# A two-layer graph network kernel: the second self weight's magnitudes are read earlier, and layer 1's self updates are put ahead of other vector work

## What is computed

```
deg_inv = 1 / max(deg, 1)                                  # deg: edges that arrive at a node
layer(h, Ws, Wn, b) = h @ Ws + (segment_sum(h[src], dst) * deg_inv[:, None]) @ Wn + b
h   = relu(layer(x, Ws0, Wn0, b0))
out = layer(h, Ws1, Wn1, b1)
result = layernorm(x + out)
```

## Time and profile before

| | |
|---|---|
| median of 3 runs | 699.4 us |
| profiled execution, device time | 701.54 us |
| its span, first to last instruction | 699.9 us |
| TensorE busy | 635.0 us (91%) |
| VectorE busy | 497.0 us (71%) |
| ScalarE busy | 274.1 us (39%) |
| GpSimd busy | 117.6 us (17%) |
| mean granted TensorE clock | 0.967 of full |

### The profile page before, as it was taken

One profiled execution on the slowest core, in us unless ns is written; L12 is line 12 of the kernel. 1 busy time (PEld: TensorE's weight loads), 2 busy tenths in 40 slices (PEclk: granted clock), 3 DMA queues, 4 the chain that ended last, 5 costly groups with the idle time before them and its releaser, 6 DMA issues.

```text
span 699.9 us, 11077 instructions
## 1 busy us (share of the span) xinstructions
PE 635.0 (91%) x3286; PEld 325.6 (47%) x3286; DVE 497.0 (71%) x1209; ACT 274.1 (39%) x492; POOL 117.6 (17%) x200
## 2 busy tenths in 40 slices
PE   3688989998999999999998999999979879879795
PEld 3644545544666666555554444444434334333242
DVE  7796487868777875398999866632029996676764
ACT  5572734343334344036444544423215331222221
POOL 3001236533233333100000000002121220000000
PEclk9799999999999999999999999999998989999998
DMA  8614000000000000333111000007724526100111
GB/s 316 236 63 178 1 1 0 0 1 1 0 1 1 0 0 0 117 126 120 60 60 32 0 1 1 0 1 248 264 91 150 178 86 242 61 31 30 61 60 54
DMA packets 16141, 50.33 MB, mean 72 GB/s; under 512 B 2616, under 2 KB 2776, under 8 KB 16096
## 3 DMA queue, kind: packets, MB, share of 16 engines
q1 hardware_dynamic: 16096, 49.77, 20.2%
HBM read 40.45 MB, written 9.31 MB: 71 GB/s over the span
## 4 chain that ended last, share of the span: by engine, by line
PE 58%; DVE 19%; issue 9%; DMA 5%; ACT 5%; SPq 1%; POOL 1%; DVEq 0%; POOLq 0%; ACTq 0%
PE ps L674 15%; PE ps L771 14%; PE ps L713 12%; PE ps L647 10%; PE ps L571 4%; DMA ws<-in_L_gnn_W_neigh 2%; DVE xz L1365 2%; ACT wn L966 2%; DMA wn<-in_L_gnn_W_self 2%; PE ps L808 2%; DVE table L1358 2%; DVE table L1340 2%; DVE wn L308 1%; DVE wn L1531 1%; DVE wn L1373 1%
## 5 line engine op out<-in xcount | busy, mean ns | idle before, releaser
L771 PE MATMUL ps<-xz,wn 128*128 128x512 f16 x600 | 137.3, 389 | 11.9 <-DVE ws L1531 6.2
L647 PE MATMUL ps<-wn,xz 128*128 128x512 f16 x480 | 116.4, 382 | 2.8 <-DVE wn L308 1.4
L674 PE MATMUL ps<-xz,ws 128*128 128x420 f16 (+1 forms) x576 | 116.1, 339 | 0.0
L836 ACT ACTIVATE scratch<-ps 128x240 uint16<-128x240 f32 x160 | 59.0, 371 | 120.3 <-PE ps L571 101.9
L1129 DVE TENSOR_SCALAR lohot<-iota_lo,table 125x128 f16<-125x128 f16 x320 | 87.8, 274 | 25.2 <-PE ps L571 24.6
L1131 DVE TENSOR_SCALAR scratch<-iota_q,table 125x240 f16<-125x240 f16 x320 | 104.5, 327 | 0.3 <-issue 0.2
L771 PEld LDWEIGHTS ps<-xz,wn 128*128 128x128 f16 x600 | 59.5, 100 | 87.3 <-DVE wn L1373 11.7
L485 POOL TENSOR_TENSOR A<-A,scratch 128x120 int32 x160 | 72.8, 455 | 138.9 <-ACT scratch L836 110.1
L808 PE MATMUL ps<-wn,A 128*128 128x512 f16 x200 | 79.1, 396 | 11.6 <-DVE scratch L1472 11.6
L713 PE MATMUL ps<-A,zh 128*128 128x420 f16 (+1 forms) x480 | 84.7, 340 | 0.0
L808 PE MATMUL ps<-ws,A 128*128 128x512 f16 x200 | 78.9, 394 | 0.0
(11 more groups left out here) (177 smaller groups left out, 658.4 us busy)
## 6 DMA issues: line engine op xcount, KB each, us to landing
ws<-in_L_gnn_W_neigh SPq DMA_DIRECT2D x16, 512.0 KB, 4.5
wn<-in_L_gnn_W_self SPq DMA_DIRECT2D x16, 512.0 KB, 5.0
zh<-in_x SPq DMA_DIRECT2D x9, 512.0 KB, 8.6
scratch<-in_x SPq DMA_DIRECT2D x9, 512.0 KB, 6.3
ws<-in_L_gnn_W_neigh SPq DMA_DIRECT2D x4, 1024.0 KB, 17.8
ws<-in_L_gnn_W_self SPq DMA_DIRECT2D x4, 1024.0 KB, 8.7
partial<-scratch SPq DMA_DIRECT2D x8, 512.0 KB, 3.8
wn<-partial SPq DMA_DIRECT2D x4, 512.0 KB, 6.9
```

Of the source, the lines that this page charges most:

```text
L647: ins = pe.matmul(ps[0:TP, 2 * r + half, :], lhs(a, k, t), w[:, k, b, half * HD:(half + 1) * HD], start=(k == 0 and a == 0 and b == 0), st ...
L674: ins = pe.matmul(ps[:, b, 0:CH[n]], ws[:, k, a, bass.ds(f * P, P)], xT[h][:, k, CO[n]:CO[n] + CH[n]], start=(k == 0 and a == 0 and h == 0 ...
L771: ins = pe.matmul(ps[:, b, :], slot[:, k, a, :], Tm[m][:, k, w, :], start=(m in (1, 2, 5) and k == 0 and a == 0 and w == 0), stop=(k == HK ...
L836: act.activation(stage[0:TP, r], ps[0:TP, 8 - banks + r % banks, 0:HN].rearrange("p (j w) -> p j w", j=JT), ACT.Copy).then_inc(counts_copi ...
```

## The change

Ws1's magnitudes are read in layer 0's aggregation, by eight loads of 512 KB into a buffer of their own, one at a time, and eight pairs of half-row sums on ScalarE, in every second unit from unit 4 on. tensor_max and scale("ws1") move into units 20 and 22, spread(3) stands right behind spread(2) on GpSimd, ahead of the memsets of h's tail. Layer 1's aggregation loses the magnitude reads (loads u = 0 to 3 and weight_sums(1, k)) and has the factor blocks from tile 0 on: t_sum4 behind tiles 0, 2, 4, 6, t_lows behind tiles 1, 3, 5, 7. In the self products the update of y comes before item_lows, finish is cut into `moments` (up to the variance) and the rest, which runs one iteration later; ScalarE's part is cut in the same way.

```diff
         def load_raw(eng, phase, u):
             slot, k = u % 2, u % HK
-            if 2 <= u < HK + 2:
-                eng.wait_ge(max_done, 2 * (HK * phase + u - 1))
+            if phase == 0 and 2 <= u < HK + 2:
+                eng.wait_ge(max_done, 2 * (u - 1))
             elif u >= HK + 2:
                 eng.wait_ge(t_low, ITEMS * (HK * phase + u - HK - 1))
...
+        def load_ws1(eng, k):
+            if k:
+                eng.wait_ge(ws1_summed, 2 * k)
+            eng.dma_start(ws1raw, Ws1[k * P:(k + 1) * P, :]).then_inc(ws1_in, 16)
# SyncE
             for u in range(2):
                 load_raw(sp, 0, u)
+            load_ws1(sp, 0)
...
                 for u in {0: (2, 3), 1: (4, 5), 3: (6,), 5: (7,)}.get(f, ()):
                     load_raw(sp, 0, u)
+                for k in {1: (1,), 2: (2, 3), 3: (4,), 4: (5,), 5: (6, 7)}.get(f, ()):
+                    load_ws1(sp, k)
...
-            for u in range(2):
+            for u in range(HK, HK + 2):
                 load_raw(sp, 1, u)
             sp.wait_ge(z_low, 4 * IT)
             for n in range(2):
                 load_x(n)
-            for u in range(2, HK):
-                load_raw(sp, 1, u)
...
-                for u in {0: (4, 5), 3: (6,), 4: (7,)}.get(n, ()):
+                for u in {1: (6,), 3: (7,)}.get(n, ()):
                     load_raw(sp, 1, u)
                 load_x(n + 2)
# GpSimd
             spread(2)
+            spread(3)
...
-            for n in range(3):
-                residual(n)
-            spread(3)
-            for n in range(3, JT):
+            for n in range(JT):
                 residual(n)
# ScalarE
+            def ws1_sums(k):
+                act.wait_ge(ws1_in, 16 * (k + 1))
+                for a in range(2):
+                    m = MC["ws1"] + 2 * k + a
+                    act.activation(ws1dump, ws1raw[:, a * HD:(a + 1) * HD], ACT.Abs,
+                                   accum_out=mx[:, m:m + 1]).then_inc(ws1_summed, 1)
+                    act.wait_ge(ws1_summed, 2 * k + a + 1)
...
                     for k in {(0, 0): (0,), (0, 1): (1,), (1, 0): (2,), (1, 1): (3,)}.get((f, n), ()):
                         weight_sums(0, k, unread)
+                    if q >= -2 and q % 2 == 0 and q < 2 * KT - 2:
+                        ws1_sums(q // 2 + 1)
...
             for k in range(HK):
-                weight_sums(1, k, unread)
-            act.wait_ge(scale_ready, 6)
-            for k in range(HK):
                 for i in range(ITEMS):
                     t_item(1, k, i)
...
-                if m == (3 if p < IT - 1 else 2):
-                    finish(2 * p)
-                if m == 4:
-                    finish(2 * p + 1)
+                if e and e - 1 in ROW7:
+                    normalize(ROW7[e - 1])
+                if e in ROW7:
+                    root(ROW7[e])
+            normalize(JT - 1)
# VectorE
+                    if (f, n) == (6, 2):
+                        dve.wait_ge(ws1_summed, 2 * KT)
+                        tensor_max("ws1", 2 * KT, MC["ws1"])
+                    if (f, n) == (7, 1):
+                        scale("ws1")
+                        signal(scale_ready)
...
             for n in range(JT):
                 y_tile(n)
-                if n == 1:
-                    dve.wait_ge(max_done, 4 * HK)
-                    tensor_max("ws1", KT, MC["ws1"])
-                if n == 2:
-                    scale("ws1")
-                    signal(scale_ready)
+                if n == 0:
                     mul("cs1", "p_h", "p_ws1", 2.0 ** -25)
-                if 3 <= n < 3 + HK:
+                if n < 2 * HK and n % 2 == 0:
                     for i in range(4):
-                        t_sum4(1, n - 3, i)
-                    t_lows(1, n - 3, range(ITEMS))
-                if n == JT - 2:
+                        t_sum4(1, n // 2, i)
+                if n < 2 * HK and n % 2 == 1:
+                    t_lows(1, n // 2, range(ITEMS))
+                if n == 2 * HK - 1:
                     dve.wait_ge(t_low, 2 * ITEMS * HK)
                     for e in range(ITEMS):
                         s_sum(1, e)
+                if n == JT - 2:
                     for e in range(ITEMS):
                         item_lows(1, e)
...
                 if e + ITEMS < NP7:
                     s_sum(1, e + ITEMS)
-                    item_lows(1, e + ITEMS)
+                if e == NP7 - 1:
+                    finish(JT - 2)
...   # wait for product e, y += product e, statistics of the half row
-                if m == (3 if p < IT - 1 else 2):
-                    finish(2 * p)
-                if m == 4:
-                    finish(2 * p + 1)
+                if e + ITEMS < NP7:
+                    item_lows(1, e + ITEMS)
+                if e and e - 1 in ROW7 and e < NP7 - 1:
+                    finish(ROW7[e - 1])
+                if e in ROW7:
+                    moments(ROW7[e])
+            finish(JT - 1)
```

More of the change, by code:

```diff
@@ L72, in gnn_kernel @@
     MADE3 = [pm for pm in ORDER7 if pm[1] in (2, 3, 7)]
+    ROW7 = {}
+    for pair in range(IT):
+        ROW7[AT7[pair, 3 if pair < IT - 1 else 2]] = 2 * pair
+        ROW7[AT7[pair, 4]] = 2 * pair + 1
     TORDER = (1, 2, 3, 7, 5, 6, 4)
@@ L154, in gnn_kernel @@
                 for r in (wsflat[:, WSCUT:], wnflat[:, JT * D:])]
+        ws1raw = wsflat[:, WSCUT + 8 * D:WSCUT + 10 * D].bitcast(F32)
+        ws1dump = scratch[:, 2520 + 2 * D:2520 + 2 * D + HD]
         tmp3 = [[scratch[:, 2520:2520 + D].bitcast(F32), scratch[:, 2520 + D:2520 + 2 * D].bitcast(F32), sums[3]],
@@ L277, in gnn_kernel @@
         t_low = sem("t_low")
+        ws1_in = sem("ws1_in")
+        ws1_summed = sem("ws1_summed")
         part_out = [sem(f"part_out{i}") for i in range(2)]
@@ L328, in raw_landed @@
         def raw_landed(eng, phase, u):
-            eng.wait_ge(raw_in[u % 2], 32 * (HK * phase + u // 2 + 1))
+            eng.wait_ge(raw_in[u % 2], 32 * ((HK // 2) * phase + u // 2 + 1))
+        def load_ws1(eng, k):
+            if k:
+                eng.wait_ge(ws1_summed, 2 * k)
+            eng.dma_start(ws1raw, Ws1[k * P:(k + 1) * P, :]).then_inc(ws1_in, 16)
         def factor(phase, k, m):
@@ L999, in z_item @@
                 if i == 0:
-                    act.wait_ge(scale_ready, 5)
+                    act.wait_ge(scale_ready, 6)
                 act.activation(z1[0][:, t, half], ps[:, 3 * (p % 2), :] if m == 4 else made[MADE3.index((p, m)) % 2],
@@ L1030, in _, with root, normalize @@
                 item(1, e)
-            def finish(n):
+            def root(n):
+                r = n % 2
+                act.wait_ge(var_ready, n + 1)
+                act.activation(ln[0:TP, r, 1:2], ln[0:TP, r, 0:1], ACT.Sqrt).then_inc(std_ready, 1)
+            def normalize(n):
                 p, r = n // 2, n % 2
                 y = yrow(p, r)
-                act.wait_ge(var_ready, n + 1)
-                act.activation(ln[0:TP, r, 1:2], ln[0:TP, r, 0:1], ACT.Sqrt).then_inc(std_ready, 1)
                 act.wait_ge(shift_ready, n + 1)
@@ L1491, in _, with moments @@
                         s_sum(1, e)
+                if n == JT - 2:
                     for e in range(ITEMS):
                         item_lows(1, e)
-            def finish(n):
+            def moments(n):
                 p, r = n // 2, n % 2
-                y = yrow(p, r)
                 dve.wait_ge(stat_ready, 4 * p + (4 if r else 3 if p == IT - 1 else 2))
@@ L1504, in finish @@
                 dve.tensor_scalar(ln[0:TP, r, 0:1], mv[0:TP, r, 1:2], 1e-5, None, ALU.add).then_inc(var_ready, 1)
+            def finish(n):
+                p, r = n // 2, n % 2
+                y = yrow(p, r)
                 dve.wait_ge(std_ready, n + 1)
```

## The result

The changed kernel takes 666.02 us (median of four runs, 665.01 to 666.35); the kernel before, beside it, 700.44. The ratio is 0.9506, with a 95% interval of 0.9483 to 0.953. The forecast was 664 us, in a range of 660 to 676. The profiled execution took 666.15 us, with a span of 664.4, against the 664.1 that the sum gave. By medians beside each other the change is worth 34.4 us, where 35.8 were forecast.

A forecast was written before the change was run, and what follows sets the result against it. TensorE was taken as the bound, waiting avoidably in layer 1's aggregation and the self products; -17.7 - 19.6 + 1.5 = -35.8 us took the span from 699.9 to 664.1 us, the median to 664, range 660 to 676.

The forecast's parts named there:

- Layer 1's aggregation, -17.7: Layer 1's aggregation falls from 104.1 to 86.4 us, TensorE's own time at full clock, with its waits covered.
- Rival D: Layer 1's aggregation: SyncE's loads 6 and 7 hold x(3) and x(5), half of the 17.7 us is kept: 673 us; chance 0.08.
- The self products, -19.6: Self products fall from 111.3 to about 91.7 us, since VectorE updates y in time for TensorE.
- allowance of 1.0 us: Self products: 1.0 us added to the 90.7 us bound, between bounds of 0 and +2.7 us for VectorE not overlapping.
- remaining handshake of 0.15 us: Self products: VectorE still waits about 0.15 us for ScalarE's high part, four times in a pair.
- VectorE is just under TensorE, at 98%: Self products: VectorE needs 17.8 us for seven iterations against TensorE's 18.1 us, so no stall.
- Rival B: Self products: VectorE's exchange with ScalarE stays, 20.3 us against 18.1 a pair, +9 us: 672 us; chance 0.14.
- Rival E: Self products: TensorE's clock stays low behind short gaps, the 6 us beyond the waits remain: 670 us; chance 0.03.
- Layer 0, +1.5: Layer 0's aggregation: ScalarE waits for Ws1's second load, VectorE falls behind, and the first neighbour product starts 1.5 us later.
- rival C: Layer 0's aggregation: ScalarE is held by Ws1's loads at each step, landing at 7.5 us: 674 us; chance 0.12.
- spread(3): Layer 0's aggregation on GpSimd: right behind spread(2), it costs under 1 us even if GpSimd must be readied again.
- The end, 8.1 us: The last 8.1 us, which hold no matmul, stay as before; the last finish still stands between two y updates.

The follow-up runs named there:

- x5: Changed kernel with Ws1's factor blocks back behind tiles 3 to 6 and raw loads 6 and 7 behind tiles 3 and 4: 667.14 us, ratio 0.954.
- x6: Changed kernel with one more, unused GpSimd partition reduction between residual(2) and residual(3): 665.76 us, ratio 0.9519.
- x7: Changed kernel with both the factor blocks back behind tiles 3 to 6 and an unused GpSimd reduction ahead of residual(3): 674.02 us, ratio 0.9634.
- x12: x7 plus six unused 256-KB loads ahead of x(2), two at a time, each pair waited for, so x(2) comes late: 682.26 us, ratio 0.9775.
- x9: Changed kernel with one extra, unused 128x128 VectorE multiplication ahead of each y update in the self products: 666.35 us, ratio 0.952.
- x1: Changed kernel with the old self-product order: item_lows ahead of the y update, finish in one piece: 687.43 us, ratio 0.9834.
- x4: Changed kernel with item_lows back ahead of the y update in the self products, finish still cut in two: 680.07 us, ratio 0.9745.
- x11: The changed kernel run once more, unchanged: 665.56 us, ratio 0.951 to the kernel before.
- x10: x8 plus the operands of layer 1's first two products made in the last units of layer 0's aggregation: 662.23 us, ratio 0.946.
- x8: Changed kernel with Ws1's first pair of sums in unit 2 instead of 4 and its load 1 issued earlier: 662.12 us, ratio 0.948.

## Why the prediction was right

- **Layer 1's aggregation, -17.7: measured -17.6.** 86.3 us for 400 matmuls, clock 1.00, no wait on y_tile. The two places where SyncE's queue holds x for a raw load exist and are covered. Rival D (half of the gain kept back there) is out.
- **What carried it.** The prediction read the late x, the spread and the longest wait as one chain, but gave the later waits to the factor blocks by themselves. x5 has these blocks without the rest and waits 0.9 us; x6 has the reduction without the rest and doesn't wait. x7 and x12 show that they cost when they come together.
- **The self products, -19.6: measured -20.5.** The term was mis-sized by its allowance of 1.0 us, which wasn't needed: 90.7 us, the lower bound. The remaining handshake of 0.15 us was right in size (0.83 - 0.66 = 0.17), three times in a pair and not four. "VectorE is just under TensorE, at 98%" was right as a count, but x9 shows that part of that is waiting which shrinks when the order gets fuller; the real room is about 1 us in 18.1. Rival B (the exchange stays, 672) is out, but x1 and x4 show that its mechanism is real: with y behind item_lows it costs 15.5 us.
- **Rival E, the clock.** The 6 us in each stage beyond the waits went with the waits: x7, x12 and x1 lose 2.8, 4.9 and 6.5 us more in their stages than their waits on VectorE account for; the changed kernel, without waits, loses nothing. Read matmul by matmul they are slow starts: behind the wait of 5.16 us at tile 5 of the kernel before, matmuls start 0.43 us apart instead of 0.216, at a granted clock of 0.50 from 524.93 to 530.03 us. In its tiles 29 starts come over 0.3 us behind the one before without a wait between, 5.9 us in all, and 32 in its self products, 6.1 us; the changed kernel has none in either stage. Rival E (a clock that stays low behind short gaps) is out, since no gap is left to stay low behind.
- **Layer 0, +1.5: measured +2.8 (99.1 against 96.3).** Mechanism and place were right (a wait at the second load of Ws1, 4.45 us instead of about 3.5, as that load took 5.7 us and not 4.7 behind a raw load; the pair of sums 1.5 us, as estimated; VectorE 1.87 us late at the last unit; and no wait for a load at the later sums, so rival C is out). Mis-sized is the end of it: TensorE starts its first product behind a wait of 4.58 us instead of 2.44, 2.1 us later where 1.5 were forecast, and its twelve matmuls then take 5.28 instead of 4.44 us, at starts 0.43 us apart and so twice the 0.216 of full clock. The prediction priced nothing for the clock. How much that is changes from one execution to the next: in x11, the same kernel, the wait is 4.36 us, the twelve take 4.38, and the stage is 1.9 us longer than before, not 2.8.
- **spread(3)** waits for nothing of its own: it starts at 374.99 us, 0.1 us behind tensor_max's end, and VectorE never waits for it. The forecast (under 1 us) was right; the last section has the rows.
- **The end, 8.1 us,** unchanged as forecast.

The errors are +0.1, -0.9 and +1.3 us. They nearly cancel, so the sum is closer (664.1 against a span of 664.4) than the terms are. That is luck, as is the start of the two profiled executions, which moves by more than the 0.3 us and happened to be alike (layer 0's aggregation ends at 380.3 and 380.1 us). The median was forecast less well, 664 against 666.02: the prediction took the profiled execution to lie 2.1 us above the median, and the changed kernel's lies 0.1 above its own.

## What to carry to other kernels

When a stage waits in several places in one chain, ask of each link how much cover it eats, not how long it takes: with two links a removed one may bring the whole gain, and one restored alone may cost nothing, as with the reduction here (0.1 us alone, some 7 with late blocks). Where an engine that is not full holds another up, look for the exchange in the middle of its iteration and put the work that others wait for into it; that moved 15.5 us without removing one instruction. The read added to a full stage cost here at its first buffer turn and nowhere else, so try to issue the first turn early.

## What the runs showed of the hardware

- GpSimd pays for a change between a partition reduction and tensor_tensor both ways. The profile shows no work of it for 5.80, 6.43, 6.13 and 5.90 us ahead of the reduction, and for 7.18, 7.70, 7.05 and 6.99 us behind it (before, x6, x7, x12). Each of these gaps starts with two MODIFY_POOL_CONFIG of GpSimd's sequencer, in the kernel before at 507.9 and 513.8 us:

```profile
L510 POOLq MODIFY_POOL_CONFIG  x8: 11/11/11, 18.3 to 507.9; - x8
L542 POOLq MODIFY_POOL_CONFIG  x4: 11/47/83, 370.4 to 513.8; - x4
```

  From the second of them to the reduction and back to tensor_tensor pass the 5.57 and 7.11 us of the earlier trace rows. In the changed kernel none stand between spread(2) and spread(3), which follows its input at once (0.1 us), and none between spread(3) and the MEMSET behind it, which starts without a gap:

```profile
374.99 0.77 POOL L525 PARTITION_ALL_REDUCE S<-S  x1 [53.76 <-DVE S L1178]
375.63 0.59 POOL L551 MEMSET zh<- 128x30 f32 x8
```

  The Trainium skill (GPSIMD Engine Reference, "2.1 Instruction dispatch") has about 6 us for the first call to a freshly loaded GpSimd kernel. The trace agrees ahead of the reduction (5.57 us); the way back takes longer (7.11 us).
- A VectorE operation of 0.74 us that meets a GpSimd residual takes 2.84, and the residual 2.85 instead of 2.35.
- What a stall costs TensorE beyond itself isn't told by its length alone. Twelve matmuls took 2.75 us behind a wait of 0.88 us (x10), as they do at full clock, and 4.44 behind 2.44 (x8). But they took 4.38 us behind 4.36 (x11), 5.28 behind 4.58 (changed, the same kernel) and 5.28 behind 3.78 (x4):

```profile
384.20 4.38 PE L784 MATMUL ps<-xz,wn 128*128 128x512 f16 x12 [4.36 <-DVE wn L1398]
```

```profile
383.47 5.28 PE L784 MATMUL ps<-xz,wn 128*128 128x512 f16 x12 [3.78 <-DVE wn L1398]
```
